# Decoder layer with eight experts on one core: second expert layer in 512-column products, mixed in among the first layer's, and the rounding of the hidden values moved to ScalarE

## What is computed

```python
logits = jnp.einsum('bsd,de->bse', x, Wg) + bg
topk_vals, topk_idx = jax.lax.top_k(logits, TOP_K)          # 2 of 8 experts
topk_w = jax.nn.softmax(topk_vals, axis=-1)
h = jax.nn.relu(jnp.einsum('bsd,edf->bsef', x, W1) + b1)    # 256 -> 512
eo = jnp.einsum('bsef,efd->bsed', h, W2) + b2               # 512 -> 256
...
mixed = jnp.sum(sel * topk_w[..., None], axis=2)
y = mixed + x
...
return gamma * (y - mu) * jax.lax.rsqrt(var + LN_EPS) + beta
```

## Time and profile before

| | us |
|---|---|
| median of 3 runs (868.5 to 870.71) | 870.52 |
| the profiled execution's own time | 872.48 |
| its span, from first to last instruction | 870.6 |
| PE busy (x4756) | 759.8, 87% |
| DVE busy (x1087) | 637.3, 73% |
| ACT busy (x936) | 467.3, 54% |
| POOL busy (x249) | 309.1, 36% |
| mean granted TensorE clock | 0.948 |

### The profile page before, as it was taken

How to read it: one execution, slowest core, us unless ns; L and a number is a source line. 1 busy time by engine, 2 the same in 40 slices (tenths; PEclk the granted TensorE clock), 3 DMA queues, 4 the chain that set the end, 5 groups by cost and what they waited for, 6 DMA issues and landing times.

```text
span 870.6 us, 15055 instructions
## 1 busy us (share of the span) xinstructions
PE 759.8 (87%) x4756; PEld 381.7 (44%) x4756; DVE 637.3 (73%) x1087; ACT 467.3 (54%) x936; POOL 309.1 (36%) x249
## 2 busy tenths in 40 slices
PE   6789999999999998998988978989789899999810
PEld 3442222222222222222223446666578677777710
DVE  3488888887888887886875889688837445788755
ACT  2225677767777766776776635252334344445422
POOL 8000600000000597970002475465712654533321
PEclk9798999999999999999999999888889999999965
DMA  7746040130403589891000270000231322412121
GB/s 197 180 108 159 2 92 19 27 82 3 92 19 69 154 256 292 224 254 63 2 1 1 91 296 1 0 2 1 73 129 54 105 92 84 155 48 81 56 98 48
DMA packets 51747, 80.76 MB, mean 93 GB/s; under 512 B 16532, under 2 KB 35479, under 8 KB 50777
## 3 DMA queue, kind: packets, MB, share of 16 engines
q1 hardware_dynamic: 37641, 44.91, 18.9%
q0 software_dynamic: 9952, 31.29, 11.7%
q10 hardware_dynamic: 4080, 3.61, 1.7%
HBM read 48.21 MB, written 33.11 MB: 93 GB/s over the span
## 4 chain that ended last, share of the span: by engine, by line
PE 58%; DVE 22%; DMA 7%; issue 5%; ACT 3%; POOL 3%; SPq 1%; DVEq 0%; POOLq 0%; ACTq 0%
PE bank L542 11%; PE bank L534 11%; PE quad L515 10%; PE quad L857 7%; DVE rowmax L932 6%; PE bank L871 5%; DMA kstack<-k_parts 3%; PE bank L466 2%; PE quad L612 2%; PE bank L644 2%; ACT probs L1460 2%; DVE sc L1035 1%; DVE sum L1047 1%; DVE max L1042 1%; DMA qstack<-q_parts 1%
## 5 line engine op out<-in xcount | busy, mean ns | idle before, releaser
L932 DVE TENSOR_REDUCE rowmax<-quad 128x1 f32<-128x1024 f32 x256 | 303.1, 1219 | 81.3 <-PE quad L515 80.9
L1460 ACT ACTIVATE probs<-bank 128x512 f32<-128x512 f32 x512 | 284.2, 595 | 117.7 <-PE bank L534 115.0
L534 PE MATMUL bank<-qstack,kstack 98*128 98x512 bf16 x512 | 194.0, 387 | 14.2 <-ACT probs L1460 10.2
L515 PE MATMUL quad<-kstack,qstack 96*128 96x512 bf16 x512 | 178.1, 388 | 15.9 <-DMA qstack<-q_parts 6.5
L542 PE MATMUL bank<-probs,v_all 128*32 128x512 f32 x1024 | 139.0, 611 | 0.0
L534 PEld LDWEIGHTS bank<-qstack,kstack 98*128 98x128 bf16 x512 | 49.0, 97 | 193.8 <-ACT probs L1460 161.3
L857 PE MATMUL quad<-xbT,w 128*128 128x128 bf16 x1104 | 92.9, 219 | 8.5 <-issue 5.0
L857 PEld LDWEIGHTS quad<-xbT,w 128*128 x1104 | 76.4, 97 | 25.6 <-issue 16.7
L1795 POOL DMA_INDIRECT y_tokens<-ysb,dest x46 | 50.5, 1097 | 90.7 <-DVE ysb L1175 79.8
L515 PEld LDWEIGHTS quad<-kstack,qstack 96*128 96x128 bf16 x512 | 48.6, 99 | 77.6 <-DVE rowmax L932 36.2
L1574 ACT ACTIVATE xbT<-bank 128x512 bf16<-128x512 bf16 x46 | 27.4, 597 | 92.6 <-PE bank L838 79.6
(11 more groups left out here) (180 smaller groups left out, 976.7 us busy)
## 6 DMA issues: line engine op xcount, KB each, us to landing
xb<-x_sorted SPq DMA_DIRECT2D x46, 129.0 KB
x_sorted<-blank POOLq DMA_DIRECT2D x6, 774.0 KB, 10.2
w1raw<-in_w POOLq DMA_DIRECT2D x8, 512.0 KB, 6.4
w2raw<-in_w POOLq DMA_DIRECT2D x8, 512.0 KB, 7.0
w_split<-w1two POOLq DMA_DIRECT2D x8, 512.0 KB, 6.2
w_split<-w2two POOLq DMA_DIRECT2D x8, 512.0 KB, 4.6
w<-w_split SPq DMA_DIRECT2D x16, 256.0 KB, 5.0
w<-w_split SPq DMA_DIRECT2D x8, 512.0 KB, 9.7
```

Of the source, the lines that this page charges most:

```text
L515: mm = pe.matmul(bank[2 * (p % 2) + e], q, kstack[slot][0:MAXROW, j, e * 512:e * 512 + 512], start=True, stop=True)
L534: mm = pe.matmul(bank[4 + i % 2], kstack[slot][0:KROWS, j, kt * P:kt * P + P], qstack[slot][0:KROWS, half, j, :], start=True, stop=True)
L932: dve.tensor_reduce(rowmax[:, k % 2, p:p + 1], quad[:, 2 * (p % 2):2 * (p % 2) + 2, :].rearrange("p a n -> p (a n)"), AX_X, ALU.max).then_ ...
L1460: act.activation(probs[:, i % PR, :], bank[4 + i % 2], ACT.Exp, scale=INV4).then_inc(probs_ready, 1)
```

## The change

Five things are done together.

1. `w2`'s high and low part lie side by side, 2 x 256 columns for an expert. The product of `hh` with both is one matmul of 512 columns; `hl` with the high part stays one of 256. The second layer is 8 matmuls rather than 12, with 3 computed addresses rather than 7. Its PSUM bank then holds two sums of 256 columns, and DVE adds the second in a further instruction (`keep_y`, with the semaphore `y_begun` between the two). SP loads w2 in 4 transfers of twice the size.
2. On PE the first six products of block m+2's first layer stand alone; the other 18 are mixed in among the 8 of block m's second layer.
3. The expert's offset for block m+3 is read in the middle of that mixture, not ahead of the first layer. Before the first block three offsets are read in a row. The waits on `xbT_done` in `turn_block` and on `hid_done` in `hidden` go, and that on `start_done` stays once for each half.
4. ACT makes `hh` (`high_hidden`), after the copy of the next turned block; that copy comes one block later in ACT's program (`keep_block(m + 2)` rather than m + 3).
5. On DVE the extras of a group are cut into seven pieces, one for each block, the first at m = 28: two halves of `mix`, moments, `centre`, `first_norm`, moments, `last_moments`. ACT finishes the tiles in two pairs.

```diff
@@ before.py
-        w2d = nc.dram_tensor("w2_split", (P, 2 * FC, NE, D), BF16, kind="Internal").ap()
+        w2d = nc.dram_tensor("w2_split", (P, FC, NE, 2 * D), BF16, kind="Internal").ap()
...
-        w2 = [[sb(f"w2_{half}_{fc}", [P, NE * D], BF16) for fc in range(FC)] for half in range(2)]
+        w2 = [sb(f"w2_{fc}", [P, NE * 2 * D], BF16) for fc in range(FC)]
...
-        MIX, FIRST, LAST = (HB + 6, HB + 12), (HB + 9, HB + 15), (HB + 12, HB + 18)
+        MIX = (HB + 5, HB + 12)
...
             def turn_block(m):
 
                 pe.wait_ge(xb_loaded[m % XB], 16 * (m // XB) + 16)
-                if m >= 2:
-                    pe.wait_ge(xbT_done, m - 1)
-                else:
+                if m < 2:
                     pe.wait_ge(pT_done, 3 * NT - 1 + m)
...
+            def load_start(m):
 
                 h, i = m // HB, m % HB
-                pe.wait_ge(start_done, h + 1)
-                at = pe.value_load(start_of[0:1, h, i:i + 1], min_val=0, max_val=(NE - 1) * P)
+                if i == 0:
+                    pe.wait_ge(start_done, h + 1)
+                return pe.value_load(start_of[0:1, h, i:i + 1], min_val=0, max_val=(NE - 1) * P)
+
+            def start_hidden(m):
...
                 pe.wait_ge(xbT_done, m + 1)
-                if m >= 3:
-                    pe.wait_ge(hid_done, FC * (m - 2))
-                else:
+                if m < 3:
                     pe.wait_ge(logits_taken, max(m + 1, 2))
...
+            def output(m, at, step):
+
+                fc, a = step // 2, (hh, hl)[step % 2]
+                n = 2 * D if a is hh else D
+                mm = pe.matmul(bank[Y_BANK[m % 2]][:, 0:n], a[:, m % 2, fc, :], w2[fc][:, bass.ds(at * (2 * D // P), n)],
+                               start=(step == 0), stop=(fc == FC - 1), skip_group_check=True)
+                if step == YSTEPS - 1:
+                    mm.then_inc(y_ready, 1)
+
+            HSTEPS, YSTEPS, ALONE = 6 * FC, 2 * FC, 6
             turn_block(0)
             turn_block(1)
-            starts = [hidden(0)]
+            starts = [load_start(m) for m in range(3)]
+            start_hidden(0)
+            hidden(0, starts[0], range(HSTEPS))
             project_o2(TG - 1)
...
             for m in range(BLOCKS):
                 if m + 3 < BLOCKS:
                     turn_block(m + 3)
                 if m + 2 < BLOCKS:
-                    starts.append(hidden(m + 2))
-                output(m, starts.pop(0))
+                    start_hidden(m + 2)
+                    hidden(m + 2, starts[m + 2], range(ALONE))
+                start_output(m)
+                for step in range(YSTEPS):
+                    if m + 2 < BLOCKS:
+                        mixed_in = [ALONE + (HSTEPS - ALONE) * k // YSTEPS for k in (step, step + 1)]
+                        hidden(m + 2, starts[m + 2], range(*mixed_in))
+                    output(m, starts[m], step)
+                    if step == YSTEPS - 2 and m + 3 < BLOCKS:
+                        starts.append(load_start(m + 3))
...
             def split_hidden(m):
 
-                dve.wait_ge(hid_done, FC * m + FC)
+                dve.wait_ge(hh_done, m + 1)
                 if m >= 2:
                     dve.wait_ge(y_ready, m - 1)
-                dve.tensor_copy(hh[:, m % 2, :, :], hid[:, m % 2, :, :]).then_inc(hh_done, 1)
-                dve.wait_ge(hh_done, m + 1)
...
                 dve.tensor_tensor(ysb[:, m % YB, :], bank[Y_BANK[m % 2]][:, 0:D],
-                                  b2[:, bass.ds(e, 1), :].rearrange("p o d -> p (o d)"), ALU.add).then_inc(y_done, 1)
+                                  b2[:, bass.ds(e, 1), :].rearrange("p o d -> p (o d)"), ALU.add).then_inc(y_begun, 1)
+                dve.wait_ge(y_begun, m + 1)
+                dve.tensor_tensor(ysb[:, m % YB, :], bank[Y_BANK[m % 2]][:, D:2 * D], ysb[:, m % YB, :], ALU.add).then_inc(y_done, 1)
...
+            def high_hidden(m):
+                act.wait_ge(hid_done, FC * m + FC)
+                if m >= 2:
+                    act.wait_ge(y_ready, m - 1)
+                act.activation(hh[:, m % 2, :, :], hid[:, m % 2, :, :], ACT.Copy).then_inc(hh_done, 1)
...
             for m in range(BLOCKS):
                 relu(m)
-                if m + 3 < BLOCKS:
-                    keep_block(m + 3)
+                if m + 2 < BLOCKS:
+                    keep_block(m + 2)
+                high_hidden(m)
```

More of the change, by code:

```diff
@@ L413, in _ @@
             for dst, src in w_all:
[L414 removed]
+                sp.dma_start(dst[:, :], src).then_inc(w_loaded_all, 16)
             def load_block(m):
@@ L849, in hidden, with start_output @@
                 pe.wait_ge(xbT_done, m + 1)
-                if m >= 3:
-                    pe.wait_ge(hid_done, FC * (m - 2))
-                else:
+                if m < 3:
                     pe.wait_ge(logits_taken, max(m + 1, 2))
[L854 to L862, removed]
+            def hidden(m, at, steps):
+                terms = [(half, part, c) for c in range(C2) for half, part in ((0, 0), (0, 1), (1, 0))]
+                for step in steps:
+                    fc, k = step // len(terms), step % len(terms)
+                    half, part, c = terms[k]
+                    mm = pe.matmul(bank[m % 3][:, fc * P:(fc + 1) * P], w1[half][c][fc][:, bass.ds(at, P)],
+                                   xbT[:, m % 3, 2 * part + c, :], start=(k == 0), stop=(k == len(terms) - 1))
+                    if step == HSTEPS - 1:
+                        mm.then_inc(h_ready, 1)
+            def start_output(m):
                 pe.wait_ge(hl_done, m + 1)
@@ L868, in output @@
                     pe.wait_ge(y2_done, NT)
-                terms = [(a, half, fc) for fc in range(FC) for a, half in ((hh, 0), (hl, 0), (hh, 1))]
-                for k, (a, half, fc) in enumerate(terms):
-                    mm = pe.matmul(bank[Y_BANK[m % 2]][:, 0:D], a[:, m % 2, fc, :],
-                                   w2[half][fc][:, bass.ds(at * (D // P), D)], start=(k == 0), stop=(k == len(terms) - 1))
-                mm.then_inc(y_ready, 1)
+            def output(m, at, step):
[6 more added lines that the diff above has]
+            HSTEPS, YSTEPS, ALONE = 6 * FC, 2 * FC, 6
             turn_block(0)
             turn_block(1)
-            starts = [hidden(0)]
+            starts = [load_start(m) for m in range(3)]
+            start_hidden(0)
+            hidden(0, starts[0], range(HSTEPS))
             project_o2(TG - 1)
             turn_block(2)
-            starts.append(hidden(1))
+            start_hidden(1)
+            hidden(1, starts[1], range(HSTEPS))
             for m in range(BLOCKS):
@@ L1175, in keep_y, with mix @@
                 dve.tensor_tensor(ysb[:, m % YB, :], bank[Y_BANK[m % 2]][:, 0:D],
-                                  b2[:, bass.ds(e, 1), :].rearrange("p o d -> p (o d)"), ALU.add).then_inc(y_done, 1)
-            def mix(g):
+                                  b2[:, bass.ds(e, 1), :].rearrange("p o d -> p (o d)"), ALU.add).then_inc(y_begun, 1)
+                dve.wait_ge(y_begun, m + 1)
+                dve.tensor_tensor(ysb[:, m % YB, :], bank[Y_BANK[m % 2]][:, D:2 * D], ysb[:, m % YB, :], ALU.add).then_inc(y_done, 1)
+            def mix(g, j=None):
                 h = g // 2
-                for n in range(4 * g, 4 * g + 4):
+                tiles = range(4 * g, 4 * g + 4) if j is None else range(4 * g + 2 * j, 4 * g + 2 * j + 2)
+                for n in tiles:
                     if h:
@@ L1187, in mix @@
                 link(ins)
-                for n in range(4 * g, 4 * g + 4):
+                for n in tiles:
                     ins = dve.scalar_tensor_tensor(acc[:, n, :], yg[:, n % HT, 1, :], gw[:, n, 3:4], acc[:, n, :], ALU.mult, ALU.add)
-                ins.then_inc(mixed, 1)
+                if j != 0:
+                    ins.then_inc(mixed, 1)
             def normalise(u):
@@ L1700, in split_weights @@
                 raw, two, src, dst = WEIGHTS[k]
+                n, q = (2 * C2 * FC, P) if k == 0 else (FC, 2 * D)
+                high, low = (two[:, i, :] if k == 0 else two[:, :, :].rearrange("p h n -> p (h n)").rearrange("p (c h d) -> p c h d", h=2, d=D)[:, :, i, :] for i in range(2))
+                raw = raw[:, :] if k == 0 else raw[:, :].rearrange("p (c d) -> p c d", d=D)
                 m = 2 * e + k
```

50 lines of the change are left out of this document (26 added, 24 removed).

## The result

The change takes the kernel from 869.51 us (866.22 to 870.71, four runs) to **859.16 us** (854.54 to 862.02, four runs): ratio 0.9887, 95% interval 0.9855 to 0.9918. It is faster, but by 10 us and not by the 24 of the forecast, and 859.16 lies 1.2 above the end of its range. The profiled execution took 857.96, its span 856.1.

The account below looks back on a forecast made before the run. The prediction took PE's sequencer, issuing addresses and offset reads, to bound the steady block loop, and DVE where extras run. Its stage terms summed to -23.7 us, taking the profiled 872.48 to 848.8 and the median to 846.8; range 841 to 858.

Parts of the forecast that it names:

- The steady iteration, 3.2: Block loop, iterations 12 to 27: PE's sequencer sets 3.2 us each, 0.69 less than before, 11.0 in all.
- Mixing is what lets the two overlap: PE's block loop: long products run while short ones' addresses are made; sequencer 3.21 us, PE 2.87 per iteration.
- DVE. The cast goes ... the second addition comes: equal: DVE's block loop: 0.45 for the cast leaves, 0.46 for the second addition comes; 1.75 us per loop.
- no cast that takes 2.85: Sign of success on DVE: the trace after the change would show no cast as long as 2.85 us.
- the path: From the first layer's end over ACT's relu and copies to `hl` on DVE: 3.2 us, slack 0.5 before PE waits.
- The second rival: Block loop: ACT's copy too long or DVE late to `hl`, iterations 3.6, saving 12.5 us to 858; chance 0.16.
- The first rival: First layer on PE: weight loads pace short products, iteration about 3.6, saving 12.0 us to 858.5; chance 0.09.
- The extras: Iterations 28 to 41: DVE sets the pace, extras cut into seven pieces, 50.0 us in all, 6.7 less.
- The start: Before iteration 0: three offset reads in a row delay the first product, adding 1.3 us.
- The near transfer: Block 23's load behind the last scatter: 0.2 to 0.5 us spare; a miss costs not over 1 us, once.
- The end: Iteration 42 to PE's last product: 10.2 us; with the second addition's 0.46 behind it, 1.5 less.
- Iterations 7 to 11: Block loop: 0.69 less per iteration, 3.4 us in all, with the 2.7 us excess left as it was.

Follow-up runs that it names:

- d_two_reads: a_dve_beta with the expert's offset read twice per iteration, the second result unused; 869.22 us, ratio 0.9985 to the kernel before the change.
- d_unmixed: a_dve_beta with all 24 first-layer products ahead of the second layer, as before the change; 848.68 us, ratio 0.9782 to the kernel before.
- d_dve_hh: a_dve_beta with `hh` made by DVE ahead of `hl`, not by ACT; 860.57 us, ratio 0.9872 to the kernel before the change.
- b_no_beta: The kernel before the change with POOL's four beta additions cut to one column, so part of the computation is missing; 866.36 us, ratio 1.0001.
- p_alone24: The changed kernel, POOL's additions kept, with all 24 first-layer products ahead of the second layer; 848.91 us, ratio 0.975 to the kernel before.
- p_alone15: The changed kernel, POOL's additions kept, with 15 first-layer products ahead of the wait for `hl`, not 6; 857.64 us, ratio 0.9855 to the kernel before.
- w_dve_beta: The kernel of a_dve_beta run a second time, in another series; 852.88 us, ratio 0.9789 to the kernel before the change.
- a_dve_beta: The changed kernel with the beta additions in sixteen pieces on DVE and none on POOL; 845.28 us, ratio 0.9736 to the kernel before.
- d_start: a_dve_beta with only the first block's offset read ahead of the first product, two behind its first layer; 851.63 us, ratio 0.9786 to the kernel before.

## Why the prediction was wrong, step by step

- **The steady iteration, 3.2: right**, 3.19 measured, and by the cause named, the sequencer. Four addresses cost 0.53 (forecast 0.46), a read 0.66 (0.80), so the terms were off by small amounts that cancel; the two waits that went were not measured alone. The 512-column product starts 0.22 after its neighbour, ACT's copy takes 0.65 (0.63). d_two_reads confirms the pace-setter by itself.
- **"Mixing is what lets the two overlap": wrong.** d_unmixed has the same 3.2, so the sequencer's steps set the pace in either order; what mixing did was to put the wait for `hl` early. In iterations 0 to 6 the order ate the gain: 28.9, against a forecast of 27.0 and 26.1 unmixed.
- **"DVE. The cast goes ... the second addition comes: equal", and "no cast that takes 2.85": this is the step that failed.** I read 2.85 as a property of the cast that would leave with it. It was the price of POOL's addition to whatever DVE runs then. The earlier trace rows shows 2.85 for an operation that usually takes 0.43, and the question "who holds it?" was not put. The rows of L1803 on POOL, 2.4 us four times, each starting 0.2 after a long cast and ending 0.3 before it, would have answered. `hl` stood at 0.8 in the path, with a slack of 0.5; four times it needed 3.5. So the terms of iterations 12 to 27 (-11.0, measured -2.1) and 28 to 41 (-6.7, measured -3.2) both lack it. With the additions away they measure -11.4 and -6.7 (62.26 - 50.89, 56.72 - 50.05).
- **The whole account.** The profiled execution took 857.96 for the 848.8 of the forecast, 9.2 more. By stages, measured less forecast: +8.9 in iterations 12 to 27 and +3.5 in 28 to 41 (the step above), +1.6 at the start, +1.9 in iterations 0 to 6, +0.9 at the end, -2.7 in 7 to 11, and -4.9 ahead of the first turned block. The last two are not the change's (below).
- **The second rival** ("DVE comes late to `hl`", 858) came nearest the time, by luck, though it was right that `hl` would be waited for. But it had every iteration at 3.6. Four are at 5.4 to 7.1 and the others of the steady stage at 3.2.
- **The first rival (weight load), and its rule: out.** The iteration is 3.19 where it had 3.6; the short products among long ones stand 0.056 apart.
- **The extras: right** in size, 50.1 and 49.6 against 50.0 once POOL is out of the way. That DVE sets the pace there is borne out by its 92% (45.41 of 49.56) and by d_dve_hh, where one cast more in each loop costs 6.8. That it comes of cutting the extras into seven was not tested alone.
- **The start: mis-sized only by what lies around it**; the reads cost 1.1, forecast 1.3. **The near transfer** caused no wait: iteration 20, which turns block 23, takes 3.20. **The end:** 10.7 from iteration 42 to PE's last product, forecast 10.2.
- **Iterations 7 to 11:** 3.19 each now. The excess that I left as it was belonged to the single execution, not to the kernel (below); between two profiles without it the stage goes from 19.46 to 15.96, 3.5 less, forecast 3.4.
- The 4.9 us by which the span is shorter ahead of the first turned block (639.2 to 634.3) are not the change's: that point lies anywhere from 632 to 638 in the profiles of the variants, and at 632.0 in b_no_beta, which has the old order.

## What to carry to other kernels

When one instruction in a trace takes several times its usual time, find what ran on the other engines in those microseconds before you count its removal as a gain: what held it will hold the next one. A wait that is moved ahead uses up slack that may have been hiding rare, long delays, so look at the longest instance of the awaited work and not at its mean. And before an order is made more intricate to overlap two things, check that the old order did not overlap them already.

## What the runs showed of the hardware

**An addition on POOL stops some of DVE's work, and not all.** While L1840 ran, DVE's operations with two inputs in SBUF stood still: `hl` went from 0.69 to 3.46, `dest` from 0.21 to 1.12; so did, before the change, the cast of f32 to bf16, from 0.43 to 2.85. Those with an operand in PSUM went on at 0.42 (L1193 and L1196 in the rows of p_alone24, both inside POOL's 2.38). So did BATCH_NORM_STATS2 in the attention phase of the kernel before, 0.41 to 0.42 beside POOL's elementwise operations of 2.25. The Trainium skill names it ("GPSIMD Engine Reference", Specifications): GpSimd's SBUF interfaces are shared with VectorE, with contention against instructions in a 2-port mode or with two SBUF inputs. The rows of `hl` and `dest` agree; in which mode the cast runs, no row shows. The runs add the size: beside an addition of 2.38 the cast took 2.42 longer and `hl` 2.77, beside a piece of 256 columns `hl` took 0.5 longer. POOL pays too there: 0.73 for a piece alone, 1.18 to 1.22 where it meets `hl`.

**The clock.** Behind idle stretches of PE of 2.06, 2.43 and 2.42 us the granted clock was 0.5 for 3.4 us each; behind the first, of 2.09, it stayed at 1.00, and so it did behind those of 1.4 to 1.7 in p_alone15. Iterations 24, 26 and 28, with the fall, last 1.4 to 1.7 more than iteration 22 without it.

**Products whose completion is seen late.** In nine of the fourteen profiles, the kernel before among them and all eight of the last two series, some of the iterations 7 to 12 are longer, the longest 4.7 to 5.2. ACT in w_dve_beta there:

```profile
684.27 1.14 ACT L1621 ACTIVATE hid<-quad,b 128x128 f32<-128x128 f32 x4 [2.65 <-remote]
...
689.01 1.14 ACT L1621 ACTIVATE hid<-quad,b 128x128 f32<-128x128 f32 x4 [2.59 <-remote]
```

The first layer whose end releases the relu at 684.27 was done at 681.8. POOL and DVE, which wait for PE's same completions, go on in that moment too, and PE itself runs on until its own wait. In iterations 7 to 11 it costs 2.7 us in the kernel before (22.11 to 19.46 in b_no_beta) and 5 to 7 in the versions whose steady iteration is 3.2. In the kernel before it shows on the turned blocks, whose copies start 1.0 to 1.6 after PE's last transpose where 0.04 is usual. It is most of the difference between a_dve_beta (iterations 7 to 11 in 15.94) and its repeat (20.97); it also lifts p_alone15, d_start and d_unmixed. It is not tied to any edit made here: the same kernel runs without it as a_dve_beta and with it as w_dve_beta. The four profiles of the first series have none of it and the eight of the other two all do, and each series had its own chip. Whether the chip decides was not tested. What delays the completions was not found, and stays open.
